# Edge feature projections moved from attention to the start of stage one, in twenty chunks kept in DRAM

## What is computed

```python
ep = ef @ We + be                                # 40000 x 64 @ 64 x 32
scores = einsum("ehd,ehd->eh", q[dst], k[src] + ep[:, None, :]) * scale
scores = scores * ew[:, None]
ex = exp(scores - segment_max(scores, dst)[dst])
out = segment_sum((ex / segment_sum(ex, dst)[dst])[:, :, None] * v[src], dst)
```

## Time and profile before

| | |
|---|---|
| median of three runs | 1725.58 us (1723.24 to 1728.3) |
| profiled execution, first to last instruction | 1668.6 us |
| PE, DVE, ACT, POOL busy | 1495.7, 1028.6, 615.6, 781.2 us |
| granted TensorE clock, mean | 0.923 of full |
| stages (from the trace) | tables to 188 us, stage one 194 to 812, attention 817 to the end |

### The profile page before, as it was taken

One profiled execution on the slowest core, in us unless ns is written; L12 is line 12 of the kernel. 1 busy time (PEld: TensorE's weight loads), 2 busy tenths in 40 slices (PEclk: granted clock), 3 DMA queues, 4 the chain that ended last, 5 costly groups with the idle time before them and its releaser, 6 DMA issues. The chain is left out here.

```text
span 1668.6 us, 23723 instructions
## 1 busy us (share of the span) xinstructions
PE 1495.7 (90%) x6795; PEld 1005.9 (60%) x6795; DVE 1028.6 (62%) x2542; ACT 615.6 (37%) x1534; POOL 781.2 (47%) x738
## 2 busy tenths in 40 slices
PE   4999788999999999998356799999999999999996
PEld 2554314665666777777233467767766767767785
DVE  6543244345445555545388789898898888896432
ACT  3121002333234343443022355554555445555341
POOL 1100277646755777600378666574746556540000
PEclk9999857999999999999556699999999999999997
DMA  8448456546766566631487885665757565641100
GB/s 258 164 161 261 142 151 172 154 115 191 213 175 180 166 190 178 164 94 47 137 252 216 267 253 165 193 180 167 208 152 212 143 196 169 179 122 39 29 7 9
DMA packets 191573, 270.07 MB, mean 162 GB/s; under 512 B 28295, under 2 KB 156035, under 8 KB 188867
## 3 DMA queue, kind: packets, MB, share of 16 engines
q1 hardware_dynamic: 148419, 144.77, 27.7%
q0 software_dynamic: 43008, 123.61, 26.8%
HBM read 196.22 MB, written 72.06 MB: 161 GB/s over the span
## 5 line engine op out<-in xcount | busy, mean ns | idle before, releaser
L1890 POOL DMA_INDIRECT att_kv<-table_kv,g_srcI x314 | 368.5, 1174 | 246.4 <-issue 180.4
L1149 POOL DMA_INDIRECT ex_hg<-table_h,z_idx x314 | 316.7, 1008 | 150.2 <-issue 84.9
L2441 PE MATMUL att_psR<-g_mw,att_h 128*128 128x256 f32 x640 | 163.9, 403 | 1.0 <-ACT att_h L2259 1.0
L2414 PE MATMUL att_psR<-att_t,g_mw 128*128 128x256 f32 (+1 forms) x640 | 154.8, 387 | 0.1
L1466 PE MATMUL ex_psG<-ex_hg,ex_oh 128*42 128x256 f32 x628 | 134.6, 427 | 13.3 <-DMA ex_hg<-table_h,z_idx 7.2
L751 PE MATMUL tab_psH<-e_u,tab_xT 128*128 128x512 f32 x320 | 142.6, 598 | 4.3 <-DVE e_u L532 4.3
L2441 PEld LDWEIGHTS att_psR<-g_mw,att_h 128*128 128x128 f32 x640 | 124.7, 200 | 23.0 <-ACT att_h L2259 4.0
L1387 ACT ACTIVATE ex_h<-ex_psH,g_cols 128x256 f32<-128x256 f32 (+1 forms) x240 | 97.3, 464 | 93.8 <-PE ex_psH L1488 93.1
L2414 PEld LDWEIGHTS att_psR<-att_t,g_mw 128*128 128x128 f32 x640 | 121.2, 199 | 16.6 <-issue 2.6
L1882 POOL DMA_DIRECT2D table_o<-att_part x59 | 54.2, 919 | 161.9 <-DMA table_o<-att_part 90.5
L2301 PE MATMUL att_psG<-att_kv,att_oh 128*42 128x264 f32 x628 | 109.5, 431 | 13.7 <-DVE att_kv L1997 13.3
(11 more groups left out here) (308 smaller groups left out, 2465.1 us busy)
## 6 DMA issues: line engine op xcount, KB each, us to landing
table_h<-tab_hs SPq DMA_DIRECT2D x20, 1024.0 KB, 4.0
att_eft<-in_eft SPq DMA_DIRECT2D x158, 64.0 KB
ex_db<-table_dst SPq DMA_DIRECT2D x79, 126.0 KB
table_ohT<-ex_ohT SPq DMA_DIRECT2D x79, 126.0 KB
att_ohT<-table_ohT SPq DMA_DIRECT2D x79, 126.0 KB
table_oh<-ex_oh SPq DMA_DIRECT2D x79, 84.0 KB, 2.3
att_oh<-table_oh SPq DMA_DIRECT2D x79, 84.0 KB, 4.0
table_kv<-ex_qkv SPq DMA_DIRECT2D x10, 512.0 KB, 4.8
```

Source lines behind the costliest of these rows:

```text
L1149: nc.gpsimd.indirect_dma_start(hg[:, t % RING0, :], None, d.h[:, :], bass.IndirectOffsetOnAxis(ap=g.idx0[:, t:t + 1], axis=0)).then_inc(go ...
L1890: nc.gpsimd.indirect_dma_start(kv[:, t % (RINGC * TP), H:H + 2 * D], None, d.kv[:, :], bass.IndirectOffsetOnAxis(ap=g.srcI[:, t:t + 1], ax ...
L2414: ins = nc.tensor.matmul(out[:, c * CB:c * CB + used(b)], g.mw1[:, e, k, c * P:(c + 1) * P], t3[:, k, 0:used(b)], start=(k == 0), stop=(k ...
L2441: ins = nc.tensor.matmul(out[:, q * D:(q + 1) * D], h1[:, n % 3, k, q * P:(q + 1) * P], g.mw2[:, e, k, :], start=(k == 0), stop=(k == DK - 1))
```

## The change

`features` leaves attention. In stage one PE now makes the projections of four groups (`EC`) at once, a chunk: eight matmuls of the same shape into one `psH` buffer, 512 columns. Twenty chunks (`NEC`) stand in the order at 2.3 + 1.2 c. ACT empties each with one copy into a ring of three (`epK`), SP stores it in DRAM (`d.ep`), and in attention SP loads one chunk per four groups into `epb`, from which DVE's `add` reads directly. SP loads the chunks' features in stage one into a ring of six (`EIN`), four of which lie in the space of the feed-forward weights `f1` and `f2`, loaded later. The `If` on the flag, with both copies of SP's program, moves from attention to stage one. The weights `We` are loaded at the start of stage one and no longer beside the first sums.

```diff
+EC = 4
+NEC = -(-NG // EC)
+EIN, EOUT = 6, 3
...
+def place_ep(c):
+    return EP_AT + EP_PACE * c
+EP_AT, EP_PACE = 2.3, 1.2
 def order0(groups, engine):
     out = []
+    if groups and engine in ("PE", "ACT"):
+        out += [(place_ep(c), "ep", c, 0) for c in range(NEC)]
+    if groups and engine == "SP":
+        out += [(place_ep(c - EIN + 1) + 0.5 if c >= EIN else EP_AT + 0.9 * (c - 4), "eft", c, 0) for c in range(2, NEC)]
+        out += [(place_ep(c) + 1.2, "keep", c, 0) for c in range(NEC)]
...
+                        if what == "ep":
+                            n = min(EC, NG - EC * b) * P
+                            act.wait_ge(s.half_made, half["ep", b, 0] + 1)
+                            if b >= EOUT:
+                                act.wait_ge(ep_stored[b % EOUT], 16 * (b // EOUT))
+                            nc.scalar.copy(epK[:, b % EOUT, 0:n], psH[:, half["ep", b, 0] % 3, 0:n]).then_inc(s.half_ready, DK)
...
+                def features(c):
+                    if c == 0:
+                        pe.wait_ge(s.we_loaded, 32)
+                    n = half["ep", c, 0]
+                    pe.wait_ge(eft_got[c % EIN], 32 * (c // EIN + 1))
+                    if n >= 3:
+                        pe.wait_ge(s.half_ready, DK * (n - 2))
+                    for i in range(min(EC, NG - EC * c)):
+                        out = psH[:, n % 3, i * P:(i + 1) * P].rearrange("p (a t c) -> p a t c", a=2, c=DH)
+                        for t in range(2):
+                            ins = nc.tensor.matmul(out[:, :, t, :], eft_chunk(c)[:, i, t * P:(t + 1) * P], g.we[:, :], start=True, stop=True)
+                    ins.then_inc(s.half_made, 1)
...
+                def load_features(c, features):
+                    if c >= EIN:
+                        sp.wait_ge(s.half_made, half["ep", c - EIN, 0] + 1)
+                    n = min(EC, NG - EC * c)
+                    for a in range(2):
+                        sp.dma_start(eft_chunk(c)[a * ED:(a + 1) * ED, 0:n, :],
+                                     features[:, EC * c * TP * P:(EC * c + n) * TP * P].rearrange("f (i a q) -> f i a q", a=2, q=2 * P)[:, :, a, :]).then_inc(eft_got[c % EIN], 16)
+                def keep_features(c):
+                    n = min(EC, NG - EC * c) * P
+                    sp.wait_ge(s.half_ready, DK * half["ep", c, 0] + DK)
+                    sp.dma_start(d.ep[c * P:(c + 1) * P, 0:n], epK[:, c % EOUT, 0:n]).then_inc(ep_stored[c % EOUT], 16)
...
-                program(sp)
+                if redo:
+                    program(None)
+                else:
+                    with sp.If(sp.value_load(g.flags[0:1, 1:2], min_val=0, max_val=1)):
+                        program(d.eft)
+                    with sp.If(sp.value_load(g.flags[0:1, 0:1], min_val=0, max_val=1)):
+                        program(d.efs)
...
 SLOT1 = {
-    "PE": (("sums", -0.271), ("feat", -0.236), ("cols", -0.027), ...
+    "PE": (("sums", -0.271), ("cols", -0.027), ...
-    "ACT": (("odd", -0.123), ("exp", 0.044), ("pw", 0.245), ("feat", 0.502), ("scale", 1.507)),
+    "ACT": (("odd", -0.123), ("exp", 0.044), ("pw", 0.245), ("scale", 1.507)),
...
                 def add(i):
                     dve.wait_ge(kv_got[i % RINGC], 64 * (i // RINGC) + 16 * len(tiles(i)))
-                    dve.wait_ge(s.ep_ready, i + 1)
+                    dve.wait_ge(ep_got[i // EC % 2], 16 * (i // EC // 2 + 1))
...
-                def load_features(i, features):
-                    if i >= INS:
-                        sp.wait_ge(s.ep_made, i - INS + 1)
-                    for a in range(2):
-                        sp.dma_start(eft[a * ED:(a + 1) * ED, i % INS, :],
-                                     features[:, (2 * i + a) * (TP // 2 * P):(2 * i + a + 1) * (TP // 2 * P)]).then_inc(eft_got[i % INS], 16)
+                def load_features(c):
+                    if c >= 2:
+                        sp.wait_ge(s.added, EC * (c - 1))
+                    n = min(EC, NG - EC * c)
+                    sp.dma_start(epb[:, c % 2, 0:n, :, :].rearrange("p i t c -> p (i t c)"), d.ep[c * P:(c + 1) * P, 0:n * P]).then_inc(ep_got[c % 2], 16)
```

More of the change, by code:

```diff
@@ L1106, in stage_sums_experts @@
         for what, b, e in orders["PE"]:
-            if what in ("A", "B"):
+            if what in ("A", "B", "ep"):
                 half[what, b, e] = len(half)
-        assert [v for v in orders["PE"] if v[0] in ("A", "B")] == [v for v in orders["ACT"] if v[0] in ("A", "B")]
+        assert [v for v in orders["PE"] if v[0] in ("A", "B", "ep")] == [v for v in orders["ACT"] if v[0] in ("A", "B", "ep")]
         before, last = {}, None
@@ L1552, in program @@
                     for what, b, e in orders["PE"]:
+                        if what == "ep":
+                            features(b)
                         if what == "group":
@@ L1641, in program @@
                             load_nodes(i)
+                        for to in (g.we[0:ED, 0:DH], g.we[ED:P, DH:2 * DH]):
+                            sp.dma_start(to, d.we).then_inc(s.we_loaded, 16)
+                        for c in range(2):
+                            load_features(c, features)
                     for what, b, e in orders["SP"]:
+                        if what == "eft":
+                            load_features(b, features)
+                        if what == "keep":
+                            keep_features(b)
                         if what == "store":
@@ L1803, in stage_attention @@
         in_got = [m.cleared_sem(f"in_got{b}") for b in range(INS)]
-        eft_got = [m.cleared_sem(f"eft_got{b}") for b in range(INS)]
+        ep_got = [m.cleared_sem(f"ep_got{b}") for b in range(2)]
         oh_got = [m.cleared_sem(f"oh_got{b}") for b in range(3)]
@@ L2183, in _ @@
             def _(act):
-                def features(i):
-                    act.wait_ge(s.ep_made, i + 1)
-                    if i >= 2:
-                        act.wait_ge(s.added, i - 1)
-                    nc.scalar.copy(epb[:, i % 2, :, :].rearrange("p (a t) c -> p t a c", a=2),
-                                   psE[:, 0:P].rearrange("p (t a c) -> p t a c", a=2, c=DH)).then_inc(s.ep_ready, 1)
                 def scale(i):
@@ L2202, in program @@
                 def program(_):
-                    if not redo:
-                        features(0)
                     for what, b, e in orders["ACT"]:
@@ L2231, in program @@
                                 scale(i)
-                        if what == "feat":
-                            i, j = b, b - LAG
-                            if i + 1 < NG:
-                                features(i + 1)
                         if what == "att":
@@ L2513, in steps @@
                                     load_windows(j + 3)
-                        if what == "loadE" and b + INS < NG:
-                            load_features(b + INS, features)
+                        if what == "loadE" and b % EC == 0 and b // EC + 1 < NEC:
+                            load_features(b // EC + 1)
                         if what == "loadQ" and b + INS < NG:
```

60 lines of the change are left out of this document (25 added, 35 removed).

## The result

The changed kernel takes 1765.65 us (median of four runs, 1752.32 to 1767.04) against 1724.41 us (four runs, 1707.03 to 1728.3): ratio 1.0247, 95% interval 1.0201 to 1.0294. It is slower by some 42 us; the prediction said 1726, with a range to 1746.

A forecast was written before the change was run, and what follows sets the result against it. PE was taken to bound most of the kernel, DVE close behind in attention, with room in the half-clock first sums. Terms +21 + 0 + 0 - 18 - 3 = 0 on span 1668.6 plus 57.0 gave 1726 us, range 1711 to 1746.

The forecast's parts named there:

- the start of block 0: Stage one: 2 us gained in the first sums, 2.4 lost in SP's queue; 0 in all, bounds -2 and +5.
- attention, put at -21: Attention without features: 18 us less in the steady part and 3 us less at the start.
- The price of a chunk: PE in stage one: 1.75 us a chunk at full clock; twelve chunks among block 0's experts cost 21 us.
- The first sums: Stage one, 200 to 260 us: chunks 0 to 7 find room and raise the clock, 2 us gained by group 8.
- The rival itself: First sums: clock stays at 1.2 GHz, a chunk takes 3.64 us; +24 us, 1750 us, chance 0.13.
- SP's queue: Stage one: group 8's store, which starts block 0, waits behind chunk 5's keep and goes 2.4 us later.
- Loads and copies in stage one: SP's new loads and stores and ACT's 20 copies: nothing; contention with new loads only in block 0's upper bound.
- Attention's steady part: PE loses 27.5 us of features, 20.7 on the chain; 18 us return (12.5 to 20.7), DVE being late next.
- the first rival: Attention gives back everything it shows, 1717 us, chance 0.30; against it, DVE decides once some 26 us return.
- The second rival: Attention's second half is held by its gathers; only 12.5 us return, +8.5, 1734 us, chance 0.21.
- The boundary: Second `If` runs before attention starts instead of after it ends: a wash, 0, 2 us either way.
- the prediction's own signs of being wrong: Stage one's end moves under 10 us, clock 0.50 up to 260 us, or attention shrinks under 12 or over 28 us.

The follow-up runs named there:

- the run with the keeps moved: Changed kernel with each chunk's keep 1.2 places later in SP's order, nothing left out; ratio 1.0249 to the kernel before.
- the late chunks: Changed kernel with the twenty chunks at 12.0 + 1.2 c, all behind block 0's turn, loads and stores moved along; ratio 1.0151 to the kernel before.
- attention's part alone: Kernel before with moved If and no features in attention, which loads raw feature rows for stored projections; no chunks, feature loads or stores in stage one; ratio 0.9953.
- the idle matmuls: Unread matmuls before each block's gates turn: seven in attention alone (0.9861), changed kernel (1.0111), changed kernel with late chunks (1.0040); four in kernel before (0.9936).

## Why the prediction was wrong

Two terms of the sum failed above all: the start of block 0, put at 0, came 19.2 us late, and attention, put at -21, returned 8. The 42 us come out of the experiments as -8 for attention's part with the moved `If`, +39 for the chunks' matmuls, and, less surely, +6 for the loads (1.0023 - 0.9989) and +6 for copies, stores and the one matmul left (0.9989 - 0.9953). The shares hang on the order of leaving out: the loads alone, taken first, are worth 8 (1.0247 - 1.0202).

**The price of a chunk** was right at full clock: 1.82 us a chunk for 1.75. Twelve of them among the experts were put at 21 us and held TensorE for 24.3, since one of them still ran at 3.5 us; that the stretch from block 0's turn grew by 28.7 is within the 11 us by which it differs among executions.

**The first sums** are the first step that failed: "I expect the rise", a chunk being "a dense run of the same kind", and with it the stretch that "has room". The clock rose for some chunks only. In the changed kernel's profile four of the eight before block 0's turn ran at 3.5 us, in two other profiles with the early chunks all eight, and block 0's turn came at 293.5 to 300.6 us in these three, where the forecast had 0 later and at most 5. A run without gaps of 46 us at 0.50 shows that the rows around one rise did not carry that far. The prediction read Part 1 of the Trainium skill's page TensorE: Matmul & The Clock Gate, by which activity releases the half rate, as ruling this rival out; where TensorE was busy 45.66 of 46 us, it was not released, and the measurement decides. The rival itself (the clock stays at 1.2 GHz, +24 us, 1750) came nearest, with a chance of 0.13. Its terms were 16.5 for late sums, 4.2 for the keep's wait and 3.6 for chunk 7; in the run with the keeps moved they measure 8.4, 6.0 and 5.5 (chunks 6 and 7). It saw the mechanism, and missed what attention would keep.

**SP's queue** was the right place and the wrong size: 2.4 us were put where the store went 8.3 us after the sum instead of 0.2. The prediction saw the keep of chunk 5 before group 8's store, and not the load of chunk 11, which waits for the same chunk. It also took the chunk and its copy to follow at once; in the changed kernel ACT's copy began only at 269.34 us, 3.5 us after the chunk's matmuls, and why is not shown. Without the chunks' matmuls the store still goes 7.2 us after the sum, without loads and matmuls 2.9, with the late chunks 0.8. No run moves both keeps and loads behind the store and leaves the chunks early, so what that would win is untested.

**Loads and copies in stage one** were put at nothing in the sum, contention only into a bound; the runs put them at 1.0023 - 0.9953, some 12 us together. The profiles place most of it at the start of block 0 again, whose turn stands at 288.27 us without the matmuls and at 277.91 with attention's part alone. The DMA share of the first sums rose from 0.51 to 0.86.

**Attention's steady part** is the second step that failed: 18 us, "late next is DVE". The step looked at which engine is late next, and not at what an emptier TensorE does to its own clock. The time at half clock in the steady part was 20 us before, 41 with attention's part alone and 51 in the changed kernel. What half clock costs, four pairs of runs show: with the idle matmuls 36, 46, 41 and 15 us of it went (attention alone, the changed kernel, the late chunks, the kernel before), and 16, 23, 19 and 11 us of time. By half of the time, the 21 us that attention alone has more cost some 10; that is an estimate. The timed runs with idle matmuls on both sides give 13 in the place of 8, so 5, with a large uncertainty. Neither makes the first rival's 26 likely. The second rival's reason, gathers that hold the second half, is not seen: VectorE's wait for them, over the steady part of the changed kernel, is not larger than before:

```profile
L1982 DVE TENSOR_TENSOR att_kv<-att_kv,att_epb 128x1024 f32<-128x1024 f32 x54 | 65.6, 1215 | 10.4 <-DMA att_kv<-table_kv,g_srcI 8.3 <-issue 2.1
```

**The boundary** between the stages, set at 0 with 2 either way, grew by 5.4 us in the changed kernel. From the end of the last projections to the first gather all executions without the moved `If` take 10.6 to 10.7 us, and the two of attention's part alone, without any chunk, 14.1 and 14.2: 3.5 us come with that part, and are within its return of 8. The `If` by itself was not tried. The other 2 come with the loads: the two runs without them have 14.0 and 14.1, the other runs with chunks 16.1 to 16.4.

**The sum** was made against an execution that was no typical one. In a sum of differences that did no harm by itself, but the times of landmarks (264.8, 790, 852) were 10 to 40 us off for every later comparison, and two of the prediction's own signs of being wrong stayed silent: the clock up to 260 us was 0.60 and not 0.50, and stage one's end moved by far more than 10 us.

Left open: why some stretches of chunks raised the clock and others of the same pieces did not, and which other waits hide some 13 of the late chunks' 33.6 us.

## What to carry to other kernels

Work taken out of an engine whose clock depends on what it does is worth its full return only if the clock stays; look in the profile for the wait that the removal opens, and whether the instructions behind it become slower. If the clock is then held up by other means, do the same to the kernel that it is compared with. Room in a stretch at half clock is room at half clock: price what is moved there at that level, unless a row shows the same instructions raising it. When a piece is moved in an in-order queue, look for every piece before the one that is late which waits for the same event: moving one of two wins nothing. And before a prediction rests on one profiled execution, hold its span against the timed runs.

## What the runs showed of the hardware that was not expected

- Chunks (128x64, f32) and sums kept TensorE busy 45.66 of 46 us at a granted clock of 0.50, in the run with the keeps moved.
- Seven idle 128x256 matmuls per block brought the mean clock of attention's steady part from 0.95 and 0.97 to 0.99 and 1.00 and made the kernel 16 us faster; with a chunk of sixteen records of 128x64 in the same place, and waits of up to 1.02 us behind it, the clock fell in three of seven blocks.
- Taking 40 us of matmuls out of attention won 8 us (13 with idle matmuls on both sides), adding as many cost 23.
